# An attention kernel's last two heads: sums without transfers, tiles one at a time, output blocks behind them

## The chip, the cores and the metric

The kernel runs on one core of one Trainium2 chip. The metric is the device time of one execution in microseconds, here the median of three runs. The engines are named TensorE (PE in the profile), VectorE (DVE), ScalarE (ACT), GpSimd (POOL) and SyncE (SP, which here only issues transfers).

## What is computed

Four sequences of 2048 tokens, 512 channels, float32:

```
xn  = layernorm(x)
q   = split_heads(xn @ q_w.T + q_b, 16) / sqrt(32)     # k, v alike, not scaled
ctx = softmax(q @ k.T) @ v                             # per head, 64 heads in all
x   = x + (ctx merged) @ out_w.T + out_b + tanh(xn @ weight @ aux_weight1 @ aux_weight2 + bias)
```

## The kernel before

Two stages ahead of attention (the weights, and the projections block by block) leave q and k as a high and a low part, v, and `y` (everything of the result but the attention's share) in memory off the core. The third stage, `build_attend`, goes through 64 heads in a loop of groups of four; the last four heads (60 to 63) are written out. `more` is the number of heads that follow within the written-out part (3, 2, 1, 0 for heads 60 to 63), and 4 in the loop.

A head has 16 key tiles of 128 keys. For each tile TensorE writes four score matmuls (`scores`, L1031; a unit is one 128x512 bank) into a ring of three banks `st_bank`, ScalarE turns each into exps of `probs` (L846, in `exps`), and TensorE uses the tile (`use`, L1037: four matmuls side by side, each to 32 partitions of `pv_bank`, 8 records). For the maximum of the head after, TensorE also writes `sm_bank` (four banks, L1015), VectorE reduces it (L929), and the row of maxima is turned by TensorE (`turn_max`), negated by VectorE and sent by SyncE into the head's stack (`load_row`).

The softmax's sums: ten tiles are added by GpSimd into `pool_sum` (`add`, L781), six (`CHAINS`) by accumulating transfers into `dma_sum` (`join`, L792, issued from GpSimd's queue), then `pool_sum` is merged into `dma_sum` by one more (`merge`, L800), and TensorE sums over the partitions with a matrix of ones (`add_up`). ScalarE copies values and sums out (`copy_pv`, `copy_sums`, L853), VectorE takes reciprocals in three pieces (`recip`, L921), GpSimd scales (`scale`, L806), and SyncE stores the context (`store`, four transfers, L700). TensorE works on tiles in pairs: scores of two tiles, then the uses of the two before.

Seven of the eight `probs` buffers are reused within a head (`SLOT`); an exp that reuses one waits until the old tile is used and added. 

After the last head come 16 output blocks of 512 tokens. A block's context is loaded (L705) into the stacks of finished heads, split into `ctx_hi` (ScalarE, L864; for the first two VectorE, L970) and `ctx_lo` (VectorE, L955), multiplied by `wo_hi` and `wo_lo` in three passes (L261, 48 matmuls into four `out_banks`), `y` is added by VectorE (L963) and the result stored (L720, L717). Blocks 0 and 1 run before the last head's sums are taken from TensorE's queue, then `add_up` of head 63, then blocks 2 to 15. SyncE's queue holds head 63's store and a wait for all context stores ahead of the load of context 4. Blocks 12 to 15 are those whose sequence holds head 63.

## Time and profile before

| | |
|---|---|
| median of three runs | 4139.67 us (4138.31 to 4141.12) |
| profiled execution | 4140.99 us, span 4139.2 us |
| granted TensorE clock, mean | 0.995 |
| TensorE busy | 4072.0 us (98%) |
| VectorE busy | 3125.5 us (76%) |
| ScalarE busy | 2356.7 us (57%) |
| GpSimd busy | 3253.4 us (79%) |

The span runs from the first to the last instruction; times in the trace are counted from its start. Busy shares are means over stages with different limits. A granted clock of 1.00 is TensorE's full 2.4 GHz, half of it is the lower level of 1.2 GHz; a stretch's value is the mean over it. In a row of a timeline `xN` merges N neighbours, and a bracket gives the idle time before them and what ended it.

### The profile page before, as it was taken

The page shows a single profiled execution, that of the slowest core. Times are in us where ns is not written, and L with a number is a line of the kernel's source. Part 1 is how long each engine was busy: PE and PEld are TensorE (multiplying, and loading weights), DVE is VectorE, ACT ScalarE, POOL GpSimd, SP SyncE. Part 2 cuts the span into 40 slices and gives each one's busy share as a digit, 9 for nine tenths or more (in the row PEclk, how much of TensorE's full clock was granted, in tenths as well). Part 3 has the DMA queues.
Part 4 walks back from the last instruction along what each step waited for, and adds up shares of the span by engine and source line. Part 5 has one row for each costly group of instructions (what it writes and reads, how often), then busy time and mean ns, then how long its engine had stood idle before and what let it go on. Part 6 is the DMA issues. An engine that isn't in the chain of part 4 may idle for free.

```text
span 4139.2 us, 77715 instructions
## 1 busy us (share of the span) xinstructions
PE 4072.0 (98%) x21216; PEld 2495.7 (60%) x21216; DVE 3125.5 (76%) x5058; ACT 2356.7 (57%) x4515; POOL 3253.4 (79%) x1180
## 2 busy tenths in 40 slices
PE   8999999999999999999999999999999999999999
PEld 6888888755555555555555555555555555555467
DVE  4344334788888888888888888888888888888554
ACT  2222222266666666766666667666666766676621
POOL 1222222299999999999999999999999999999930
PEclk9999999999999999999999999999999999999999
DMA  4444445578888888888888887888888888888787
GB/s 170 158 167 162 152 147 169 161 149 175 174 178 172 174 170 175 170 173 176 176 176 172 174 170 167 175 175 175 179 169 176 172 173 172 176 176 173 156 263 262
DMA packets 246352, 722.11 MB, mean 174 GB/s; under 512 B 87392, under 2 KB 88416, under 8 KB 184544
## 3 DMA queue, kind: packets, MB, share of 16 engines
q0 software_dynamic: 55296, 402.68, 50.2%
q1 hardware_dynamic: 107648, 201.88, 14.4%
q10 hardware_dynamic: 83040, 113.01, 9.8%
q8 instruction: 185, 3.03, 0.3%
q14 instruction: 183, 1.50, 0.1%
HBM read 178.00 MB, written 136.31 MB: 76 GB/s over the span
## 4 chain that ended last, share of the span: by engine, by line
PE 46%; DMA 19%; issue 9%; POOL 3%; ACT 3%; POOLq 0%; ACTq 0%; SPq 0%; DVE 0%; DVEq 0%
PE sm_bank L1015 14%; PE pv_bank L1037 14%; PE st_bank L1031 14%; DMA dma_sum<-probs 11%; DMA dma_sum<-pool_sum 8%; ACT probs L846 3%; PE sm_bank L261 2%; POOL pool_sum L781 2%; PE sm_bank L1037 1%; PE st_bank L261 1%; POOL ctx_out L806 1%; PE sm_bank L1024 0%; POOL dma_sum L792 0%; DMA q_stack<-s_ctx 0%; ACTq L845 0%
## 5 line engine op out<-in xcount | busy, mean ns | idle before, releaser
L929 DVE TENSOR_REDUCE part_max<-sm_bank 128x1 f32<-128x512 f32 x4016 | 2442.1, 678 | 410.9 <-PE sm_bank L1015 404.1
L781 POOL TENSOR_TENSOR pool_sum<-pool_sum,probs 128x2048 f32<-128x2048 f32 x512 | 2504.8, 4892 | 16.6 <-ACT probs L846 0.7
L846 ACT ACTIVATE probs<-st_bank 128x512 f32<-128x512 f32 x3840 | 1959.8, 616 | 611.9 <-PE st_bank L1031 585.5
L1031 PE MATMUL st_bank<-q_stack,k_stack 97*128 97x512 f32 x4096 | 1649.2, 404 | 15.0 <-ACT probs L846 8.5
L1015 PE MATMUL sm_bank<-k_stack,q_stack 96*128 96x512 f32 x4016 | 1655.5, 412 | 5.3 <-issue 2.8
L1015 PEld LDWEIGHTS sm_bank<-k_stack,q_stack 96*128 96x128 f32 x4016 | 764.8, 190 | 551.9 <-DVE part_max L929 331.7
L1031 PEld LDWEIGHTS st_bank<-q_stack,k_stack 97*128 97x128 f32 x4096 | 780.5, 191 | 268.4 <-ACT probs L846 127.5
L1037 PE MATMUL pv_bank<-probs,v_pairs 128*32 128x512 f32 x7680 | 934.9, 602 | 0.0
L1037 PEld LDWEIGHTS pv_bank<-probs,v_pairs 128*32 128x32 f32 x7680 | 205.5, 110 | 455.7 <-ACT probs L846 262.8
L792 POOL DMA_DIRECT2D dma_sum<-probs x320 | 348.6, 1089 | 66.0 <-ACT probs L846 28.9
L405 POOL TENSOR_TENSOR y_out<-y_out,x_in 128x512 f32<-128x512 f32 x64 | 82.8, 1293 | 369.6 <-ACT y_out L437 365.2
L781 POOL TENSOR_TENSOR pool_sum<-probs 128x2048 f32<-128x2048 f32 x64 | 330.5, 5164 | 0.1
L921 DVE RECIPROCAL ratio<-sum_copy 128x168 f32<-128x168 f32 (+1 forms) x192 | 230.9, 1204 | 38.1 <-ACT sum_copy L853 38.1
L524 DVE SCALAR_TENSOR_TENSOR qk_lo<-proj,qk_bias,qk_hi 128x512 fp32r<-128x512 f32 x128 | 96.1, 751 | 195.0 <-ACT qk_hi L431 193.3
L431 ACT ACTIVATE qk_hi<-proj,qk_bias 128x512 fp32r<-128x512 f32 x128 | 88.1, 688 | 272.4 <-PE proj L261 272.4
L437 ACT ACTIVATE y_out<-y_out 128x512 f32<-128x512 f32 x64 | 40.5, 632 | 319.6 <-DVE y_out L513 319.6
L846 ACT ACTIVATE dma_sum<-st_bank 128x512 f32<-128x512 f32 x256 | 132.4, 603 | 132.4 <-PE st_bank L1031 132.3
L394 POOL TENSOR_TENSOR rstd<-rstd,power 128x4 f32<-128x4 f32 x15 | 15.3, 1017 | 190.5 <-DVE rstd L459 190.5
L513 DVE TENSOR_TENSOR y_out<-proj,row_bias 128x512 f32<-128x512 f32 x64 | 44.3, 692 | 121.8 <-PE proj L261 121.8
L853 ACT ACTIVATE sum_copy<-sm_bank 128x512 f32<-128x512 f32 x64 | 38.2, 597 | 168.9 <-PE sm_bank L1037 168.9
L502 DVE TENSOR_TENSOR v_out<-proj,row_bias 128x512 f32<-128x512 f32 x64 | 44.3, 692 | 104.7 <-PE proj L261 104.7
L806 POOL TENSOR_TENSOR ctx_out<-pv_copy,ratio 128x512 f32<-128x512 f32 x64 | 103.6, 1619 | 20.8 <-issue 20.8
(116 smaller groups left out, 3198.6 us busy)
## 6 DMA issues: line engine op xcount, KB each, us to landing
dma_sum<-probs POOLq DMA_DIRECT2D x320, 1024.0 KB, 8.3
dma_sum<-pool_sum POOLq DMA_DIRECT2D x64, 1024.0 KB, 10.2
q_stack<-s_q_hi ACTq DMA_DIRECT2D x122, 256.0 KB, 6.4
k_stack<-s_k_hi ACTq DMA_DIRECT2D x122, 256.0 KB, 4.4
x_in<-in_x SPq DMA_DIRECT2D x16, 1024.0 KB, 7.7
s_q_hi<-qk_hi SPq DMA_DIRECT2D x16, 1024.0 KB, 4.3
s_q_lo<-qk_lo SPq DMA_DIRECT2D x16, 1024.0 KB, 6.4
s_k_hi<-qk_hi SPq DMA_DIRECT2D x16, 1024.0 KB, 4.3
```

Source lines behind the costliest of these rows:

```text
L261: last = nc.tensor.matmul(out, a(c), b(c), start=(c == 0 and n == 0), stop=(c == CT - 1 and n == 2))
L431: nc.scalar.activation(qk_hi[:, t, g], proj[:, u % RING], ACT.Identity, bias=keep["qk_bias"][:, t, g:g + 1]).then_inc(hi_ready, 1)
L524: nc.vector.scalar_tensor_tensor(qk_lo[:, t, g], proj[:, u % RING], keep["qk_bias"][:, t, g:g + 1], qk_hi[:, t, g].bitcast(F32), ALU.add, ...
L781: nc.gpsimd.tensor_tensor(total[:], one[:], tile_at(r, kt)[:], ALU.add).then_inc(pool_added, 1)
L792: nc.gpsimd.dma_start(dma_sum[r % 2][:], tile_at(r, CHAINS[0][j])[:], accum_op=ALU.add).then_inc(joined[r % 2], DMA)
L806: nc.gpsimd.tensor_tensor(ctx_out[r % 2][:], pv_copy[r % 2][:], ratio[:], ALU.mult).then_inc(context_ready, 1)
L846: nc.scalar.activation(tile_at(r, kt)[:, q * BLK:(q + 1) * BLK], st_bank[:, st_place(kt * QB + q)], ACT.Exp, scale=SCALE).then_inc(probs_r ...
L921: nc.vector.reciprocal(ratio[:, columns], sum_copy[r % 2][:, columns]).then_inc(recip_ready, 1)
L929: nc.vector.tensor_reduce(part_max[:, k:k + 1], sm_bank[:, sm_place(k)], AX.X, ALU.max).then_inc(max_scores_read, 1)
L1015: nc.tensor.matmul(sm_bank[:, sm_place(k)], q_st[r][0:ROWS, q * P:(q + 1) * P], k_st[r][0:ROWS, b * BLK:(b + 1) * BLK], start=True, stop=T ...
L1031: nc.tensor.matmul(st_bank[:, st_place(u)], k_st[r][0:ROWS + 1, kt * P:(kt + 1) * P], q_st[r][0:ROWS + 1, q * BLK:(q + 1) * BLK], start=Tr ...
L1037: last = nc.tensor.matmul(bank[q * DH:(q + 1) * DH, :], left, right[:, q * BLK:(q + 1) * BLK], start=start, stop=stop)
```

## The change

The last two heads and the start of the output stage are rewritten; heads 0 to 61 keep their order except for the points named.

- **TensorE.** From tile 12 of head 62 on (`end_of_heads`, 20 steps) it takes tiles one at a time: four scores, then the use of the tile two before. The scores go round five banks (`end_ring`: three of `st_bank`, two of `sm_bank` whose maxima are over). The row of maxima for head 63 is turned at the first step.
- **Sums of head 62**: joins as before, but no merge; `add_up_both` spreads `dma_sum` and `pool_sum` by two series of matmuls.
- **Sums of head 63**: no transfers. TensorE sums seven tiles (`PE_TILES`) with ones right behind their use into the bank of the maxima (`last_sum`); GpSimd adds the other nine (`add_last`, eight adds), and `add_up_last` adds that before block 3. GpSimd's scale of head 62 stands before its fifth add.
- **Output.** The first matmul group of block 0 stands before the uses of tiles 14 and 15; blocks 0 to 3 are written out, 4 to 13 are a loop, 14 and 15 written out. Output banks, result buffers and the buffers of `y` are others.
- **SyncE.** `wo_hi` and `wo_lo` are loaded behind head 60's store instead of head 61's. Contexts 0 to 3 and `y` 0 and 1 are loaded before head 62's store. Head 63's store stands behind block 3; the wait for all context stores behind block 9, before context 12 is loaded.
- **VectorE.** Head 61's reciprocals follow the last maxima; the first two contexts are split before head 62's reciprocals; head 63's stand around results 3.

The diff, cut to its core (moved or renamed lines that the prediction doesn't speak of are left out):

```diff
--- before.py
+++ after.py
@@ -51,7 +51,17 @@
...
-RESULT_TILES = [9, 11]
...
+LAST = ALL_HEADS - 1
+END_TILE = 12
+PE_TILES = [0, 1, 2, 5, 8, 10, 13]
+LAST_POOL = [kt for kt in range(KT) if kt not in PE_TILES]
+LAST_ADDS = len(LAST_POOL) - 1
+LAST_SCALE = 4
+RESULT_TILES = [8, 10]
+EARLY_BLOCKS = 4
+LAST_CONTEXT = (BATCH - 1) * TB
...
+def in_end(h, kt):
+
+    return isinstance(h, int) and (h == LAST or (h == LAST - 1 and kt >= END_TILE))
+
+
+def end_unit(h, u):
+
+    return (h - LAST + 1) * UNITS + u - END_TILE * QB
...
-        y_in = [tiled(pool_sum[0]), tiled(q_st[3]).bitcast(F32)]
+        y_in = [tiled(pool_sum[0]), tiled(dma_sum[0])]
...
-        out_banks = [sm_bank[:, b] for b in range(SM_BANKS) if b != sm_place("sum")] + [st_bank[:, 0]]
+        last_sum = sm_bank[:, sm_place("max")]
+        out_banks = [sum_bank] + [sm_bank[:, b] for b in range(SM_BANKS) if b not in (sm_place("sum"), sm_place("max"))]
+        out_banks += [st_bank[:, 0]]
+        end_free = [max(k for k in range(UNITS) if sm_place(k) == b) for b in range(SM_BANKS)]
+        end_ring = [st_place(END_TILE * QB + i) for i in range(ST_BANKS)]
+        end_ring += [ST_BANKS + b for b in range(SM_BANKS) if b not in (sm_place("sum"), sm_place("max"))]
...
+        def score_bank(h, u):
+
+            if not in_end(h, u // QB):
+                return st_bank[:, st_place(u)]
+            place = end_ring[end_unit(h, u) % len(end_ring)]
+            return st_bank[:, place] if place < ST_BANKS else sm_bank[:, place - ST_BANKS]
...
-            def body(h, r, more, following):
-                if more == 0:
-                    for n in range(2):
-                        sp.wait_ge(lo_ready, n + 1)
-                        load_context(n + 2, n)
-                    sp.wait_ge(tile_used, PRIME + h * KT + KT)
-                    load_y(1, 1)
-                    store_result(0, 0)
-                    load_y(2, 0)
-                    store_result(1, 1)
-                    load_y(3, 1)
-                if more >= 2:
-                    load_row(following + 1, (r + 2) % GROUP)
-                if more == 1:
-                    sp.wait_ge(sums_ready, PRIME + h + 1)
-                    load_y(0, 0)
-                store(h, r)
-                if more == 2:
-                    sp.wait_ge(first["v_stored"], V_STORED)
-                    sp.wait_ge(first["y_stored"], Y_STORED)
-                    sp.dma_start(wo_hi[:].bitcast(F32), dram["wo_hi"].rearrange("(r p) c -> p r c", p=P)).then_inc(w_loaded, DMA)
-                    sp.dma_start(wo_lo[:].bitcast(F32), dram["wo_lo"].rearrange("(r p) c -> p r c", p=P)).then_inc(w_loaded, DMA)
-                    for n in range(2):
-                        load_context(n, n)
-
-            heads(sp, body)
-            for s in context_stored:
-                sp.wait_ge(s, PRIME + CTX_DMAS * DMA * ALL_HEADS // 2)
-
...
-            block_pairs(sp, output)
+            def body(h, r, more, following):
+                if more >= 2:
+                    load_row(following + 1, (r + 2) % GROUP)
+                if more == 1:
+                    sp.wait_ge(sums_ready, PRIME + h)
+                    for n in range(2):
+                        load_context(n, n)
+                    for n in range(2):
+                        sp.wait_ge(lo_ready, n + 1)
+                        load_context(n + 2, n)
+                    sp.wait_ge(sums_ready, PRIME + h + 1)
+                    for n in range(2):
+                        load_y(n, n)
+                if more >= 1:
+                    store(h, r)
+                if more == 3:
+                    sp.wait_ge(first["v_stored"], V_STORED)
+                    sp.wait_ge(first["y_stored"], Y_STORED)
+                    sp.dma_start(wo_hi[:].bitcast(F32), dram["wo_hi"].rearrange("(r p) c -> p r c", p=P)).then_inc(w_loaded, DMA)
+                    sp.dma_start(wo_lo[:].bitcast(F32), dram["wo_lo"].rearrange("(r p) c -> p r c", p=P)).then_inc(w_loaded, DMA)
+
+            heads(sp, body)
+            for n in range(2):
+                store_result(n, n)
+                load_y(n + 2, n)
+            for n in range(2, EARLY_BLOCKS):
+                output(n, n % 2, True)
+            store(LAST, LAST % GROUP)
+            block_pairs(sp, output, EARLY_BLOCKS, LAST_CONTEXT - 2)
+            for s in context_stored:
+                sp.wait_ge(s, PRIME + CTX_DMAS * DMA * ALL_HEADS // 2)
+            block_pairs(sp, output, LAST_CONTEXT - 2, BLOCKS - 2)
...
+            def add_last(i):
+
+                total, kt = pool_sum[LAST % 2], LAST_POOL[i + 1]
+                if i == 0:
+                    pool.wait_ge(sums_ready, PRIME + LAST - 1)
+                pool.wait_ge(probs_ready, PRIME + LAST * UNITS + QB * (kt + 1))
+                one = tile_at(LAST, LAST_POOL[0]) if i == 0 else total
+                if i:
+                    pool.wait_ge(pool_added, PRIME + LAST * POOL_ADDS + i)
+                nc.gpsimd.tensor_tensor(total[:], one[:], tile_at(LAST, kt)[:], ALU.add).then_inc(pool_added, 1)
...
+                if more >= 2:
+                    for i in range(POOL_ADDS):
+                        if i == SCALE_ADD:
+                            scale(h, r)
                         sum_up(following, (r + 1) % GROUP, i)
-                    if i == MERGE_AFTER:
-                        merge(h, r)
+                        if i == MERGE_AFTER:
+                            merge(h, r)
+                elif more == 1:
+                    for i in range(LAST_ADDS):
+                        if i == LAST_SCALE:
+                            scale(h, r)
+                        add_last(i)
+                else:
+                    scale(h, r)
...
-                        if old in POOL_TILES:
+                        if not back and isinstance(h, int) and h == LAST:
+                            if old in LAST_POOL:
+                                act.wait_ge(pool_added, PRIME + h * POOL_ADDS + max(1, LAST_POOL.index(old)))
+                        elif old in POOL_TILES:
                             act.wait_ge(pool_added, PRIME + h * POOL_ADDS - back * POOL_ADDS + adds_after(old))
...
+                bank = last_sum if isinstance(h, int) and h == LAST else sum_bank
+                copy_bank(h, r, bank, sum_copy, sums_ready, PRIME + h + 1, sums_copied)
...
+                    high(3, 1)
...
             heads(act, body)
-            high(3, 1)
-            block_pairs(act, lambda n, par, ahead: high(n + 2, par) if ahead else None)
+            for n in range(4, EARLY_BLOCKS + 2):
+                high(n, n % 2)
+            block_pairs(act, lambda n, par, ahead: high(n + 2, par), EARLY_BLOCKS, BLOCKS - 2)
...
-                if more == 0:
+                if more >= 3:
+                    rest(following + 1, sums_of=(h, r))
+                    begin(following + 2, sums_of=(h, r))
+                elif more == 2:
+                    rest(following + 1, last=True)
+                    negate(following + 1)
+                    for piece in range(len(RECIPS)):
+                        recip(h, r, piece)
+                elif more == 1:
                     for n in range(2):
                         high(n, n)
                         low(n, n)
-                    dve.wait_ge(tile_used, PRIME + h * KT + KT)
-                    dve.wait_ge(pool_added, PRIME + h * POOL_ADDS + adds_after(RESULT_TILES[1]))
-                    results(0, 0)
-                    low(2, 0)
-                    results(1, 1)
                     for piece in range(len(RECIPS)):
                         recip(h, r, piece)
-                else:
-                    rest(following + 1, units=more >= 2, sums_of=(h, r))
-                    begin(following + 2, units=more >= 3, new=more >= 2, sums_of=(h, r))

             heads(dve, body)
+            for n in range(EARLY_BLOCKS):
+                if n:
+                    low(n + 1, (n + 1) % 2)
+                if n == EARLY_BLOCKS - 1:
+                    recip(LAST, LAST % GROUP, 0)
+                results(n, n % 2)
+            recip(LAST, LAST % GROUP, 1)
+            recip(LAST, LAST % GROUP, 2)
...
+                if not in_end(h, kt):
+                    pe.wait_ge(probs_ready, PRIME + h * UNITS + st_units_before(u))
+                else:
+                    unit = end_unit(h, u)
+                    if unit >= len(end_ring):
+                        pe.wait_ge(probs_ready, PRIME + h * UNITS + u - len(end_ring) + 1)
+                    elif unit < ST_BANKS:
+                        pe.wait_ge(probs_ready, PRIME + h * UNITS + st_units_before(u))
+                    else:
+                        pe.wait_ge(max_scores_read, PRIME + LAST * UNITS + end_free[end_ring[unit] - ST_BANKS] + 1)
+                nc.tensor.matmul(score_bank(h, u), k_st[r][0:ROWS + 1, kt * P:(kt + 1) * P],
...
+                last = spread(pv_bank, v_sb[r // 2][:, kt, (r % 2) * DH:(r % 2 + 1) * DH], tile, kt == 0, kt == KT - 1)
+                if isinstance(h, int) and h == LAST and kt in PE_TILES:
+                    if kt == PE_TILES[0]:
+                        pe.wait_ge(max_row_ready, ALL_HEADS)
+                    last = spread(last_sum, ones[:], tile, kt == PE_TILES[0], False)
+                last.then_inc(tile_used, 1)
...
+            def add_up_both(h, r):
+
+                pe.wait_ge(joined[r % 2], landed(h, len(CHAINS[0]) - 1))
+                spread(sum_bank, ones[:], dma_sum[r % 2], True, False)
+                pe.wait_ge(pool_added, PRIME + h * POOL_ADDS + POOL_ADDS)
+                spread(sum_bank, ones[:], pool_sum[r % 2], False, True).then_inc(sums_ready, 1)
+
+            def add_up_last():
+
+                pe.wait_ge(pool_added, PRIME + LAST * POOL_ADDS + LAST_ADDS)
+                spread(last_sum, ones[:], pool_sum[LAST % 2], False, True).then_inc(sums_ready, 1)
...
+            def end_of_heads():
+
+                tiles = [(LAST - 1, kt) for kt in range(KT)] + [(LAST, kt) for kt in range(KT)]
+                for i in range(END_TILE, len(tiles)):
+                    h, kt = tiles[i]
+                    for q in range(QB):
+                        scores(h, h % GROUP, kt, q)
+                    before, used = tiles[i - 2]
+                    use(before, before % GROUP, used)
+                    if i == END_TILE:
+                        turn_max(LAST, False)
+                    if h == LAST and kt == CUT - 1:
+                        add_up_both(LAST - 1, (LAST - 1) % GROUP)
...
+                if more == 0:
+                    return
                 r1 = (r + 1) % GROUP
-                for p in range(CUT // 2, KT // 2):
+                for p in range(CUT // 2, (KT if more >= 2 else END_TILE) // 2):
...
+                if more == 1:
+                    end_of_heads()
...
             pe.wait_ge(consts_ready, 1)
             heads(pe, body, extra=1)
             pe.wait_ge(w_loaded, 2 * DMA)
-            pe.wait_ge(max_row_ready, ALL_HEADS)
-            output(0, 0, True)
-            output(1, 1, True)
-            add_up(ALL_HEADS - 1, (ALL_HEADS - 1) % GROUP, 0)
-            block_pairs(pe, output)
+            pe.wait_ge(sums_copied, PRIME + LAST)
+            pe.wait_ge(lo_ready, 1)
+            output_part(0, 0, 0)
+            use(LAST, LAST % GROUP, KT - 2)
+            use(LAST, LAST % GROUP, KT - 1)
+            for j in range(1, JT):
+                output_part(0, 0, j)
+            for n in range(1, EARLY_BLOCKS):
+                if n == EARLY_BLOCKS - 1:
+                    add_up_last()
+                output(n, n % 2, True)
+            block_pairs(pe, output, EARLY_BLOCKS, BLOCKS - 2)
+            last_blocks(output)
```

## Rows read from the trace of the kernel before

**Rows 1.** Windows; busy us (and count) per engine, granted clock, DMA share, GB/s
```profile
3600.00:3647.60 47.60, 47.49 (x264) 26.56 (x263) 41.80 (x69) 33.23 (x66) 46.93 (x16) 1.00 0.89 183
3882.65:3949.07 66.42, 62.47 (x269) 20.35 (x265) 20.99 (x11) 41.48 (x82) 61.76 (x20) 0.87 0.84 204
...
3979.60:3993.00 13.40, 13.40 (x49) 10.88 (x50) 9.14 (x10) 1.91 (x1) 3.14 (x1) 0.81 0.79 274
4004.70:4135.60 130.90, 130.85 (x576) 108.13 (x576) 57.44 (x61) 21.09 (x11) 0.00 (x0) 1.00 0.81 276
```
**Rows 2.** Timeline of TensorE, last two heads: start us, us, line, operation, tiles
```profile
3882.65 0.98 PE L1031 MATMUL st_bank<-q_stack,k_stack 97*128 97x512 f32 x3
3883.92 2.46 PE L1031 MATMUL st_bank<-q_stack,k_stack 97*128 97x512 f32 x5 [0.29 <-ACT probs L846]
...
3888.16 0.28 PE L1024 MATMUL sm_bank<-ident,row_max 128*16 128x128 f32 x1
...
3936.72 3.53 PE L1037 MATMUL pv_bank<-probs,v_pairs 128*32 128x512 f32 x16
```
**Rows 3.** Timeline of ScalarE, one pair of tiles
```profile
3883.27 4.03 ACT L846 ACTIVATE probs<-st_bank 128x512 f32<-128x512 f32 x8 [1.64 <-PE st_bank L1031]
```
**Rows 4.** Chain of work that ended last: start us, us, what
```profile
3858.25 7.92 DMA dma_sum<-probs
...
3906.21 11.16 DMA dma_sum<-probs
...
3993.11 6.59 DMA q_stack<-s_ctx
...
4135.60 0.69 DVE probs L963
```
**Rows 5.** Timeline of TensorE at full clock, steady heads
```profile
3832.55 1.93 PE L1037 MATMUL pv_bank<-probs,v_pairs 128*32 128x512 f32 x16
3834.41 0.50 PE L1015 MATMUL sm_bank<-k_stack,q_stack 96*128 96x512 f32 x1
3834.75 0.40 PE L1031 MATMUL st_bank<-q_stack,k_stack 97*128 97x512 f32 x1
...
3838.34 1.92 PE L1037 MATMUL pv_bank<-probs,v_pairs 128*32 128x512 f32 x16
...
3875.49 1.04 PE L1037 MATMUL sm_bank<-dma_sum,ones 128*32 128x512 f32 x8
```
**Rows 6.** Timeline of GpSimd, from head 61's sums on
```profile
3863.40 1.48 POOL L800 DMA_DIRECT2D dma_sum<-pool_sum  x1
...
3901.73 4.78 POOL L781 TENSOR_TENSOR pool_sum<-pool_sum,probs 128x2048 f32<-128x2048 f32 x1
...
3943.17 11.50 POOL L781 TENSOR_TENSOR pool_sum<-pool_sum,probs 128x2048 f32<-128x2048 f32 x2
...
3984.77 3.14 POOL L806 TENSOR_TENSOR ctx_out<-pv_copy,ratio 128x512 f32<-128x512 f32 x1 [20.75 <-issue]
```
**Rows 7.** Window of 5 us in head 62's first half
```profile
3860.00:3865.00 5.00, 4.85 (x28) 2.33 (x27) 3.64 (x7) 2.90 (x7) 5.00 (x3) 1.00 1.04 210
```
**Rows 8.** Timeline of TensorE's weight loads: the wait of head 62's sums
```profile
3925.39 0.15 PEld L1037 LDWEIGHTS sm_bank<-dma_sum,ones 128*32 128x32 f32 x4 [0.97 <-DMA dma_sum<-pool_sum]
```
**Rows 9.** Timeline of SyncE's DMA queue: when transfers were issued
```profile
3902.05 4.27 SPq L700 DMA_DIRECT2D s_ctx<-ctx_out  x4
...
3907.43 0.52 SPq L705 DMA_DIRECT2D q_stack<-s_ctx  x1
```
**Rows 10.** Timeline of VectorE, first context blocks
```profile
3934.38 3.80 DVE L970 CAST q_stack<-q_stack 128x2048 fp32r<-128x2048 f32 x1 [2.98 <-DMA q_stack<-s_ctx]
3938.21 6.51 DVE L955 TENSOR_TENSOR k_stack<-q_stack 128x2048 fp32r<-128x2048 f32 x1
...
3981.26 3.37 DVE L921 RECIPROCAL ratio<-sum_copy 128x168 f32<-128x168 f32 x3
3984.54 2.23 DVE L955 TENSOR_TENSOR k_stack<-k_stack,q_stack 128x2048 fp32r<-128x2048 f32 x1
```

More of the change, by code:

```diff
@@ L939, in begin, with rest @@
                     maxima(s, k, units, sums_of)
-            def rest(s, units=True, sums_of=None):
+            def rest(s, units=True, sums_of=None, last=False):
                 for k in range(BEGIN, UNITS):
-                    maxima(s, k, units, sums_of)
+                    maxima(s, k, units, None if last else sums_of)
                 if units:
@@ L993, in output @@
                 results(n, par)
-            block_pairs(dve, output)
+            block_pairs(dve, output, EARLY_BLOCKS, BLOCKS - 2)
+            last_blocks(output)
         @block.tensor
@@ L1064, in both_scores @@
                     s, ahead, k0 = following + 1, 2, PER_TILE * (kt - KT + AHEAD)
-                if k0 == TURN_UNIT and more >= 1:
-                    turn_max(following, more >= 2)
+                if k0 == TURN_UNIT and more >= 2:
+                    turn_max(following)
                 for q in range(QB):
```

33 lines of the change are left out of this document (13 added, 20 removed).

## The prediction

> **What bounds the kernel now.** I read the windows by stage first, then TensorE's timeline, then the chain that ended last. The windows [rows 1] show three kinds of stretch. In a steady head TensorE is busy 47.49 of 47.60 us at granted clock 1.00, and GpSimd 46.93: the two are level. From 3882.65 to 3949.07, which the change rewrites, the granted clock is 0.87. From 4004.70 to 4135.60 twelve output blocks follow each other with no gap, 130.9 / 12 = 10.9 us each. Block 2, at 3979.60, takes 13.4 us at clock 0.81.
>
> What sets 3882.65 to 3949.07 is seen in TensorE's timeline [rows 2]. The maxima matmuls are over there. Two tiles of scores are written as three matmuls, then five at 0.49 us each, every one behind an exp that frees one of three banks; then both tiles are used. A pair lasts 3888.16 - 3882.65 = 5.51 us. ScalarE has eight exps in 4.03 us and then sits idle 1.5 to 1.6 us [rows 3], since the whole burst of uses stands ahead of the next score. Neither engine is full: each waits for the other in turn.
>
> The chain [rows 4] runs through GpSimd and the accumulating transfers into `dma_sum`, then through the store and reload of context, and from 4004.7 through TensorE alone. TensorE's work ends at 4135.60; VectorE's last add and the last store bring the span to 4139.2. Between blocks 1 and 2 TensorE is idle: blocks 0 and 1 end at 3949.07 + 2 x 10.9 = 3970.9 and block 2 starts at 3979.6 [rows 1], with one spread of sums between.
>
> **The scores and uses.** I lay the new TensorE order out from 3882.65, where the old and the new code part. It has 20 tile steps (tiles 12 to 15 of head 62, 16 of head 63): four scores, then the use of the tile two back. Prices come from full clock [rows 5]. Sixteen score matmuls and both changes of kind take 3838.34 - 3834.41 = 3.93 us; a change costs 3834.75 - 3834.41 = 0.34 us, so the others are (3.93 - 0.68) / 14 = 0.23 us. Four scores with both changes are 0.34 + 0.34 + 2 x 0.23 = 1.14 us. Two uses are 3834.41 - 3832.55 = 1.86 us, one 0.93. A step is 2.05 us (I drop the last hundredths). ScalarE needs half of 4.03, 2.0 us, so TensorE just sets the pace. Do five banks suffice? A score must wait for the exp five units back; an exp starts 0.62 us after its score [rows 2, 3], and the eight in 4.03 us are seven distances of 0.49 and one duration of 0.60. The loop of five units costs 1.25 us against 2.5 us of exps: they suffice. Twenty steps: 41.0 us.
>
> Head 63's sums for seven tiles become TensorE spreads of the same form as a use. A spread of sums took 1.04 us, the part that the next matmul does not overlap 0.97 [rows 5]: 7 x 0.97 = 6.8 us. Head 62's sums are two spreads, not one (`pool_sum` is no longer merged): 1.9 us. The use of head 63's tile 0, in the seventh step, waits for ScalarE's copy of head 62's values, which follows the exps of tile 1. TensorE comes to it at 3882.65 + 6 x 2.05 + 1.14 = 3896.1. The exps begin 0.62 us after the sixth step, at 3893.5, and end 2.1 us later, the copy half a microsecond behind: 3896.1 to 3896.2. I take 0.1 us. The last two uses are 1.9 us, the last sums' spread 1.0 us.
>
> **What must be ready in time.** GpSimd's adds of head 62 end at 3906.5 [rows 6]. Then come eight adds of head 63 at 4.78 us and one scale. Exps of tiles 10, 14 and 15 reuse slots that adds 1, 2 and 3 free, at about 3911, 3916 and 3921; by the steps they are due at 3919, 3929 and 3931. Head 63's tile 7 needs the last add of head 62, 3906.5, due at 3909. So no step waits. The scale of head 62 waits for its reciprocals, which VectorE makes behind four passes over the first context blocks (below), to about 3938; a scale and four adds later it is 3959, or 3964 at the 3.14 and 5.75 us that they took beside VectorE [rows 6]. TensorE wants the sum before block 3, at about 3969 (3934 and three blocks, and what follows). Hidden, with 5 to 10 us to spare; if that cover is gone, each microsecond counts in full.
>
> **The loads of `wo`.** SyncE issues them one head earlier, behind head 60's store. Head 61's is issued at 3902.05 + 4.27 = 3906.3 [rows 9], so head 60's ends one head of 47.6 us earlier, at 3858.7. There head 62's first join and head 61's merge are in flight and the transfer engines are saturated, share 1.04 [rows 7]. Uncontended that join took 7.92 us; with 4 MB of loads beside it a join took 11.16 [rows 4]. The merge was issued at 3863.40 [rows 6]; with the same 4 MB beside it head 62's merge, issued one add after 3906.5 and so at 3911.3, held TensorE until 3925.39 [rows 8], 14 us. Now 2 MB: head 61's merge would land between 3863.4 + 7.9 = 3871.3 and 3863.4 + 14 = 3877.4, while TensorE wants it at 3875.49. The cost is 0 to 1.9 us; I take 1.0. GpSimd loses 2 to 4 us to late joins, which the slack above mostly covers.
>
> **Contexts and `y`.** The loads of context 0 and 1 still follow head 61's store, so are issued at about 3907 as before [rows 9], but nothing large is in front of them: before, context 0 landed only when VectorE began at 3934.38 [rows 10], 27 us. Alone a load took 6.59 us [rows 4]. I expect 3914 to 3917. VectorE then splits it: 3.80 + 6.51 us while GpSimd adds, but 2.23 us for the same subtraction with GpSimd idle [rows 10]. The first block is ready at 3927, the second at 3934; TensorE wants them at 3934 and 3947. `y` is issued behind the second and lands around 3943, an estimate from that 6.59 us with two loads ahead, before block 1 needs block 0's banks.
>
> **The output stage.** Sixteen blocks of 10.9 us, 174.1 us at the finer value of 10.88 between equal matmuls. Against it stands the store of the last context. Its reciprocals follow results 3, so with block 4 starting at B they end at B + 3.1 (two of the three pieces of 3.37 us [rows 10] behind 0.7 us); the scale takes at most 3.14 us [rows 6]; four stores take 4.27 us to issue [rows 9]; only then is context 6 loaded. From such a load to the block that uses it were 4004.70 - 3993.11 = 11.6 us [rows 1, 4]. Block 6 can start at B + 22.1 at the latest and is due at B + 21.8. With a quicker scale there is nothing, with a load of 7.92 us as the join's instead of 6.59 it is 1.6 us. I take nothing, nearest to the first. The wait for all stores stands before context 12 is loaded, some 60 us later: free.
>
> **The sum.** 41.0 + 6.8 + 1.9 + 0.1 + 1.9 + 1.0 + 174.1 + 1.0 = 227.8 us after 3882.65: TensorE ends at 4110.45 in place of 4135.60, 25.15 us less, with the same tail. The profiled execution took 4140.99 us for a span of 4139.2, 1.3 us above the median of 4139.67; the difference is taken off the median: 4114.5 us.
>
> **The rivals.**
> - *The sum holds*, 4114.5 us: chance 0.61. Its own range is 4111 to 4119: without contention 4113.5, at ScalarE's 2.0 us a step 4112.5, the other way 0.9 for the `wo` loads and 1.6 for context 6, 4117.0; a microsecond or two more on both sides for the transitions.
> - *The granted clock falls in the tile-by-tile stretch too.* In [rows 1] the clock was 0.87 over 66 us in which TensorE was busy 94%, and a pair's uses took 3.53 us at the lower level (1.2 GHz) against 1.9 at 2.4 GHz [rows 2]. For it: the engine still changes kind each step and meets ScalarE closely. Against: the short waits of 0.29 us after three scores, present in every pair before the fall, are gone, and a steady head with the same kinds of matmul and no such waits holds 1.00. At 0.87 the 52.7 us of work before block 0 and for the last sums take 60.6: 4122.4 us, chance 0.17. The Trainium skill's page "TensorE: Matmul & The Clock Gate", section "A second HAM failure mode: psum-queue depth-cycling", says that micro-idles between groups of matmuls that cycle through PSUM banks make the clock swing; the rows of the pairs agree, and by that rule a five-bank ring that waits often would keep this cost.
> - *GpSimd or a transfer is late.* Joins with loads beside them, a slow context 0, or reciprocals behind VectorE's contended passes. If context 0 takes 27 us again it is split at 3934.4 + 3.8 + 2.2 = 3940.4 at the earliest, and block 0 starts 6.5 us late: 4121 us, chance 0.13. For it: the chain already runs through joins. Against: the merges and five joins of head 63 are gone from the queue. The Trainium skill's "GPSIMD Engine Reference", section "Specifications", says that GpSimd shares its SBUF interfaces with VectorE instructions that have two SBUF inputs; 6.51 against 2.23 us agrees, and by that rule the adds are slowed as well.
> - *Slower than before:* the clock stays at its lower level through the whole stretch. Uses then cost 1.77 us instead of 0.93, and the 52.7 us become about 98, so 4159 us. It decides from 25 / 0.85 = 29 us of full-clock work spent at that level. The old stretch had a quarter of its time there. Chance 0.03; 0.06 is left for a gain of the sum that other waits mostly take back, half of it within 0.2%.
>
> **The range.** 4109 to 4128 holds the first three cases and their bounds. Within 0.2% is 4131.4 to 4148.0, about what a measurement can tell from no change. Faster: 0.61 + 0.17 + 0.13 + 0.02 = 0.93; same 0.04, slower 0.03.
>
> **What would show it.** Right: clock 1.00 and TensorE over 97% busy between the first tile step and block 0; steps of 2.05 us, 3.0 with sums; block 0 starting near 3934; no idle time before block 2 or 4; a wait of about 1 us at head 61's sums. Wrong: exps that wait for `pool_sum` or for joins in head 63; TensorE waiting before the spread of the last sums or before block 6; a granted clock under 1.00 in the tile steps.

## The result and the profile after

| | kernel before | changed kernel |
|---|---|---|
| median (4 runs of each) | 4140.4 us (4138.31 to 4143.34) | 4116.7 us (4113.47 to 4121.45) |
| profiled execution, span | 4140.99, 4139.2 us | 4121.45, 4119.6 us |
| first tile step to block 0's first matmul | 66.42 us [rows 1] | 50.33 us |
| from there to the end of the span | 190.1 us (4139.2 - 3949.07) | 180.9 us |

The ratio is 0.9943, 95% interval 0.9926 to 0.996: 23.7 us less, where 25.15 were forecast, and a median of 4116.7 us for the forecast's 4114.5. The profiled execution is the slowest of its four. Its first tile step comes at 3888.41, 5.8 us later than in the profile of before; from that step to the end it needs 231.2 us against 256.55, 25.35 less. The sum is judged on that stretch; the time ahead of it is taken up at the end.

The windows of the changed kernel, which answer to [rows 1] (same columns):
```profile
3888.41:3938.74 50.33, 50.33 (x318) 19.03 (x314) 23.47 (x9) 42.15 (x82) 45.35 (x12) 1.00 0.50 126
3938.74:4116.40 177.66, 177.64 (x792) 144.46 (x792) 80.22 (x83) 27.92 (x16) 24.72 (x6) 1.00 0.79 267
```
Sixteen blocks, the last two uses and the last sums' spread follow the steps with 0.02 us of idle time, all at clock 1.00: the gap before block 2, block 2's 13.4 us and the 0.87 of [rows 1] are gone. TensorE's timeline, which answers to [rows 2, 5]; a matmul's end overlaps the next start, so steps are read from starts:
```profile
3891.70 1.06 PE L1117 MATMUL pv_bank<-probs,v_pairs 128*32 128x512 f32 x8
3892.70 0.73 PE L1111 MATMUL sm_bank<-q_stack,k_stack 97*128 97x512 f32 x2
3893.26 0.62 PE L1111 MATMUL st_bank<-q_stack,k_stack 97*128 97x512 f32 x2
3893.81 1.07 PE L1117 MATMUL pv_bank<-probs,v_pairs 128*32 128x512 f32 x8
3894.81 0.50 PE L1111 MATMUL st_bank<-q_stack,k_stack 97*128 97x512 f32 x1
...
3929.57 1.07 PE L1117 MATMUL pv_bank<-probs,v_pairs 128*32 128x512 f32 x8
3930.45 1.04 PE L1117 MATMUL sm_bank<-probs,ones 128*32 128x512 f32 x8
3931.42 0.74 PE L1111 MATMUL sm_bank<-q_stack,k_stack 97*128 97x512 f32 x2
...
3973.65 1.06 PE L1117 MATMUL sm_bank<-pool_sum,ones 128*32 128x512 f32 x8
```
A step is 3893.81 - 3891.70 = 2.11 us (2.12 over several), a use alone 3892.70 - 3891.70 = 1.00. With sums behind it a use takes 0.88 and the sums 0.97, so a spread adds 0.86. No row has a bracket: the last sums' spread did not wait. GpSimd and VectorE say why, against [rows 6, 10]:
```profile
3917.75 16.73 POOL L855 TENSOR_TENSOR pool_sum<-pool_sum,probs 128x2048 f32<-128x2048 f32 x3
3941.30 1.28 POOL L844 TENSOR_TENSOR ctx_out<-pv_copy,ratio 128x512 f32<-128x512 f32 x1 [6.83 <-issue]
3942.54 20.73 POOL L855 TENSOR_TENSOR pool_sum<-pool_sum,probs 128x2048 f32<-128x2048 f32 x4
```
```profile
3918.76 4.67 DVE L1032 CAST q_stack<-q_stack 128x2048 fp32r<-128x2048 f32 x1 [24.33 <-DMA q_stack<-s_ctx]
3923.46 6.57 DVE L1017 TENSOR_TENSOR k_stack<-q_stack 128x2048 fp32r<-128x2048 f32 x1
3929.95 5.61 DVE L1032 CAST q_stack<-k_stack 128x2048 fp32r<-128x2048 f32 x1
3935.59 2.29 DVE L1017 TENSOR_TENSOR k_stack<-k_stack,q_stack 128x2048 fp32r<-128x2048 f32 x1
3937.80 3.37 DVE L983 RECIPROCAL ratio<-sum_copy 128x168 f32<-128x168 f32 x3
```
Context 0 is there at 3918.76. GpSimd's three adds beside VectorE's passes take 5.6 us each (16.73 / 3), then GpSimd waits 6.83 us for the reciprocals; its last four adds, during which VectorE is busy less than half of the time, take 5.2 each. GpSimd ends at 3963.27 and the sum is wanted at 3973.65. SyncE's queue, which answers to [rows 9]:
```profile
3908.57 4.18 SPq L735 DMA_DIRECT2D s_ctx<-ctx_out  x4
3912.79 0.97 SPq L740 DMA_DIRECT2D q_stack<-s_ctx  x1
...
3992.12 1.74 SPq L735 DMA_DIRECT2D s_ctx<-ctx_out  x4
3994.43 0.43 SPq L740 DMA_DIRECT2D q_stack<-s_ctx  x1
```
Context 0 needs 3918.76 - 3912.79 = 6.0 us from issue, where 27 us passed before. The four stores of head 63 take 1.74 us to issue, not 4.27.

### The profile page after: what moved, and what is told of

The parts are those of the page before. It is cut to its first block, busy times and chain, and to the rows that moved or that the text cites. A ratio compares the mean times of both kernels' runs of the same rounds, so it can differ in the third digit from the quotient of the medians.

```text
span 4119.6 us, 77775 instructions
## 1 busy us (share of the span) xinstructions
PE 4060.4 (99%) x21280; PEld 2484.5 (60%) x21280; DVE 3122.5 (76%) x5058; ACT 2357.2 (57%) x4515; POOL 3243.9 (79%) x1172
## 4 chain that ended last, share of the span: by engine, by line
PE 46%; DMA 19%; issue 10%; ACT 3%; POOL 2%; POOLq 0%; ACTq 0%; DVE 0%; DVEq 0%
PE sm_bank L1086 13%; PE pv_bank L1117 13%; PE st_bank L1111 13%; DMA dma_sum<-pool_sum 10%; DMA dma_sum<-probs 9%; PE sm_bank L281 3%; ACT probs L905 3%; PE sm_bank L1117 2%; PE st_bank L281 1%; POOL pool_sum L819 1%; POOL ctx_out L844 1%; POOL dma_sum L830 0%; PE sm_bank L1095 0%; PE sm_bank L1111 0%; ACTq L904 0%
## 5 line engine op out<-in xcount | busy, mean ns | idle before, releaser
L819 POOL TENSOR_TENSOR pool_sum<-pool_sum,probs 128x2048 f32<-128x2048 f32 x504 | 2462.7, 4886 | 17.6 <-ACT probs L905 2.2
L1111 PE MATMUL st_bank<-q_stack,k_stack 97*128 97x512 f32 x4064 | 1628.9, 402 | 11.7 <-ACT probs L905 5.4
L1111 PEld LDWEIGHTS st_bank<-q_stack,k_stack 97*128 97x128 f32 x4064 | 772.2, 190 | 251.3 <-ACT probs L905 114.2
L844 POOL TENSOR_TENSOR ctx_out<-pv_copy,ratio 128x512 f32<-128x512 f32 x64 | 102.0, 1594 | 32.5 <-issue 32.5
```

What stands on the lines that cost most here:

```text
L819: nc.gpsimd.tensor_tensor(total[:], one[:], tile_at(r, kt)[:], ALU.add).then_inc(pool_added, 1)
L844: nc.gpsimd.tensor_tensor(ctx_out[r % 2][:], pv_copy[r % 2][:], ratio[:], ALU.mult).then_inc(context_ready, 1)
L1111: nc.tensor.matmul(score_bank(h, u), k_st[r][0:ROWS + 1, kt * P:(kt + 1) * P], q_st[r][0:ROWS + 1, q * BLK:(q + 1) * BLK], start=True, sto ...
```

## The experiments

"Stretch" is first tile step to block 0's first matmul, "rest" from there to the end of the span. A ratio is to the kernel before on the same chip. Stretch, rest and clock are read from one profiled execution of each kernel. The edits are shown against the changed kernel, cut to the lines that matter.

**The changed kernel again** (c1), no edit.

> The changed kernel once more, for a tighter ratio and to see what its first profile can't tell: that execution was the slowest of four, and one head ahead of all changed code had a 4.1 us wait on ScalarE. If that wait is chance, this profile has none before head 61, and the span is 4 to 6 us shorter (4113 to 4116). If the new code brings it, it stands at the same head again. From the first score of tile 12 of head 62 to block 0: 50.3 us as before, plus or minus 0.5.

Measured: median 4118.98 us of six (4109.94 to 4123.74), ratio 0.9941 (0.9925 to 0.9957); stretch 50.22, rest 181.0, clock 1.00. In the three profiles of this kernel (the changed kernel's, c1 and f2 below) the stretch is 50.21 to 50.33 us and the rest 180.9 to 181.0, while the spans are 4115.6 to 4120.4: what differs between these executions lies ahead of the stretch. The wait of ScalarE that the expectation asks about is there again, at the same head (the last section).

**Three banks** (c2): the steps stay, the ring shrinks.
```diff
-        end_ring += [ST_BANKS + b for b in range(SM_BANKS) if b not in (sm_place("sum"), sm_place("max"))]
```


> Tile by tile, but the scores go round three banks as before the change. If the ring's length sets the pace: the fourth score waits for the first exp, so a step is 1.27 to that score, 0.31 and 0.93, 2.51 us in place of 2.12; 20 steps are 8 us longer, about 58 us to block 0. If ScalarE or TensorE sets the pace whatever the banks: no more than 1 us longer. If short waits of this kind bring the granted clock down: 58 us and 5 to 8 more, clock 0.87 to 0.90 in the stretch.

**Pairs, five banks** (c3): the order of before, the rest of the change as it is.
```diff
-                for i in range(END_TILE, len(tiles)):
-                    h, kt = tiles[i]
-                    for q in range(QB):
-                        scores(h, h % GROUP, kt, q)
-                    before, used = tiles[i - 2]
-                    use(before, before % GROUP, used)
+                for i in range(END_TILE, len(tiles), 2):
+                    for h, kt in tiles[i:i + 2]:
+                        for q in range(QB):
+                            scores(h, h % GROUP, kt, q)
+                    for before, used in tiles[i - 2:i]:
+                        use(before, before % GROUP, used)
```


> Five banks, but tiles in pairs: eight scores, then two uses. If the banks do it: the eighth score waits for the third exp, 2.25 us after the first; with 0.31 and 1.86 a pair is 4.42 to 4.5 us in place of 4.24, so 2 to 3 us more over ten pairs, about 53 us to block 0. If the order tile by tile does it, a pair costs 5.5 us as before the change: 13 us more. Clock 1.00 by the first.

**Pairs, three banks** (c4): both edits.

> Pairs and three banks, that is the scores and uses as before the change, with all the rest of the change (sums, output blocks, transfers) kept. A pair is 5.5 us in place of 4.24: 12.7 us more, 63 us to block 0, and with the clock falling as it did before 4 to 8 us more. The rest of the gain, about 25 less 13 to 20 us, must then stay: 5 to 12 us faster than the kernel before. If instead the order of scores is worth little, it stays within 3 us of the changed kernel.

| | median us | ratio (95%) | stretch | rest | clock in the stretch |
|---|---|---|---|---|---|
| c1 tiles, 5 banks | 4118.98 | 0.9941 (0.9925 to 0.9957) | 50.22 | 181.0 | 1.00 |
| c2 tiles, 3 banks | 4131.25 | 0.9969 (0.9958 to 0.998) | 61.43 | 181.0 | 1.00 |
| c3 pairs, 5 banks | 4123.97 | 0.9954 (0.9939 to 0.9969) | 52.93 | 181.0 | 1.00 |
| c4 pairs, 3 banks | 4134.56 | 0.9984 (0.9972 to 0.9995) | 62.73 | 180.95 | 1.00 |

The stretch as a window in c2, c3 and c4, one block each, and TensorE's timeline in c2:
```profile
3888.41:3949.84 61.43, 55.53 (x317) 18.93 (x313) 22.53 (x11) 42.29 (x82) 57.68 (x16) 1.00 0.56 159
```
```profile
3884.16:3937.09 52.93, 52.93 (x317) 20.72 (x314) 23.04 (x10) 41.34 (x82) 46.88 (x13) 1.00 0.50 126
```
```profile
3886.82:3949.55 62.73, 59.81 (x318) 20.69 (x314) 26.67 (x11) 41.24 (x82) 54.17 (x15) 1.00 0.56 157
```
```profile
3893.79 0.97 PE L1110 MATMUL st_bank<-q_stack,k_stack 97*128 97x512 f32 x3
3895.05 0.50 PE L1110 MATMUL st_bank<-q_stack,k_stack 97*128 97x512 f32 x1 [0.30 <-ACT probs L904]
3895.49 1.06 PE L1116 MATMUL pv_bank<-probs,v_pairs 128*32 128x512 f32 x8
3896.49 0.96 PE L1110 MATMUL st_bank<-q_stack,k_stack 97*128 97x512 f32 x3
```
The banks carry it: with pairs, two more are worth 62.73 - 52.93 = 9.8 us, with tiles 61.43 - 50.22 = 11.2. Tile order is worth 1.3 us with three banks and 2.7 with five. The medians differ from c1's by 12.3 us (c2), 5.0 (c3) and 15.6 (c4); the intervals of the ratios are 9 to 13 us wide, so they bear the order out, but not the single microseconds, which rest on one profile each. c3 shows no idle time, 52.93 of 52.93 us busy. Rows of TensorE's uses and of its weight loads (PEld) show where a pair loses time all the same:
```profile
3891.38 1.92 PE L1117 MATMUL pv_bank<-probs,v_pairs 128*32 128x512 f32 x16
...
3895.83 1.93 PE L1117 MATMUL pv_bank<-probs,v_pairs 128*32 128x512 f32 x16
```
```profile
3894.42 0.19 PEld L1111 LDWEIGHTS st_bank<-q_stack,k_stack 97*128 97x128 f32 x1 [0.19 <-ACT dma_sum L905]
3894.91 0.19 PEld L1111 LDWEIGHTS st_bank<-q_stack,k_stack 97*128 97x128 f32 x1 [0.30 <-ACT dma_sum L905]
3895.39 0.19 PEld L1111 LDWEIGHTS sm_bank<-q_stack,k_stack 97*128 97x128 f32 x1 [0.30 <-ACT dma_sum L905]
```
The weight loads of the sixth, seventh and eighth score of a pair start 0.48 to 0.49 us apart, which is the pace of the exps, where scores that don't wait start 0.23 apart; idle time of 0.19 to 0.30 us stands before each and ends with an exp. A pair takes 3895.83 - 3891.38 = 4.45 us where two steps take 4.24. In c2 a step is 3896.49 - 3893.79 = 2.70 us, more than the 2.51 that was expected, and its stretch 61.43 us for 58: each fourth score waits 0.30 us for an exp, and starts 1.26 us after the first where 0.34 + 2 x 0.23 = 0.80 would do. The other part of the miss was not taken apart. c4 against the kernel before is what the rest of the change gives (sums, output order, transfers, and the clock that came with them), and it is read with the next two runs.

**The kernel before again, and pairs without TensorE's sums** (d1, no edit, and d2; one execution each, as are d3 and d4 below). d2 is c4 without the seven spreads of head 63, so its sums for head 63 lack these seven tiles.
```diff
-                    last = spread(last_sum, ones[:], tile, kt == PE_TILES[0], False)
```


> The kernel before once more, for its profile: where its granted clock falls. If the fall belongs to what TensorE does there, the clock is again 0.80 to 0.90 between the first pair without maxima and block 0 (66.4 us in the first profile), and block 2 follows at about 0.8. If it was chance, the clock is 1.00 there and the stretch 60 to 62 us.

> Pairs and three banks once more, and TensorE's seven spreads of head 63's sums are left out (its softmax sums then hold GpSimd's nine tiles alone; part of the computation is missing). The run with the spreads held clock 1.00 at the same short waits. If the spreads kept it up, by filling the stretch, the clock now falls some 20 us into the stretch as in the kernel before, to 0.85 to 0.93 over it, and the stretch is 58 to 62 us in place of 62.7 - 6.8 = 55.9. If the accumulating transfers or their waits brought it down before, the clock stays at 1.00 and the stretch is 55.9 us.

Measured: d1 4138.81 us (another execution of the kernel before, timed beside d1 to d4, took 4144.79), stretch 64.05; d2 4126.53 us, stretch 63.31, rest 181.0. Windows of d1, then windows and one pair's uses of d2:
```profile
3880.82:3900.00 19.18, 18.04 (x83) 6.56 (x79) 2.96 (x5) 14.66 (x30) 18.89 (x6) 1.00 0.55 111
3900.00:3910.00 10.00, 9.23 (x35) 2.99 (x38) 0.00 (x0) 6.06 (x12) 10.00 (x6) 0.71 0.79 158
```
```profile
3880.40:3900.00 19.60, 18.45 (x84) 6.74 (x80) 3.56 (x4) 15.10 (x31) 19.31 (x7) 1.00 0.50 102
3900.00:3943.71 43.71, 41.92 (x178) 13.06 (x178) 23.18 (x7) 26.21 (x53) 35.35 (x9) 0.84 0.57 181
```
```profile
3925.91 3.36 PE L1116 MATMUL pv_bank<-probs,v_pairs 128*32 128x512 f32 x16
```
Both hold 1.00 up to 3900 and fall behind it. d2 has no joins for head 63, so joins are not needed for a fall. Against c4 it has 7 x 0.86 = 6.0 us less to do and takes 0.6 us more: the work that was taken out came back as clock, 0.89 for 1.00, with uses of 3.36 us.

Do the seven spreads keep the clock up, then? Shorter windows of the kernel before and of d2, and the first spread in c4's timeline, say only in part:
```profile
3902.00:3904.00 2.00, 2.00 (x10) 0.63 (x14) 0.00 (x0) 1.77 (x4) 2.00 (x2) 0.69 1.07 217
```
```profile
3904.00:3906.00 2.00, 2.00 (x5) 0.74 (x4) 0.00 (x0) 2.00 (x6) 2.00 (x2) 0.94 0.91 206
3906.00:3908.00 2.00, 2.00 (x13) 0.46 (x16) 0.00 (x0) 1.03 (x3) 2.00 (x1) 0.50 0.52 128
```
```profile
3907.82 1.04 PE L1116 MATMUL sm_bank<-dma_sum,ones 128*32 128x512 f32 x8
```
A mean of 0.94 or 0.69 between the levels 1.00 and 0.50 puts the fall at 3905.8 in d2 and at 3902.8 in the kernel before. So in d2 the clock falls 25.4 us after the first tile step, where c4 already has spreads behind it (the first 3907.82 - 3886.82 = 21.0 us after the step). In the kernel before and in d1 it falls after 19.9 to 20.1 us, and neither c4 nor d2 falls there, with the same order of scores and uses, the same short waits, and no spread of head 63 yet. So the spreads may account for d2 against c4, but not for the first fall of the kernel before; what spared c4 and d2 that one is open, and the joins and the other transfers that they lack remain a rival. With one profile of each of c4 and d2, chance in when the clock falls is not ruled out either, and c4's ten executions have mean granted clocks from 0.995 to 0.999, of which the profiled one is among the highest: the others may have lost clock here or elsewhere.

**The last sums before block 1** (d4): is GpSimd's cover real, and what does it cost if it is gone?
```diff
-                if n == EARLY_BLOCKS - 1:
+                if n == 1:
```


> GpSimd's part of head 63's sums is asked for before block 1, not before block 3, that is 21.8 us earlier. In the changed kernel's profile GpSimd ended 24.5 us after block 0's start and was asked after 35.0 us. If TensorE's queue order is the cover, it now waits 24.5 - 13.2 = 11.3 us before block 1, the granted clock falls for the start of block 1 (2 to 3 us more, as at block 2 of the kernel before), and the span grows by 11 to 14 us. If GpSimd speeds up without VectorE beside it, 8 to 11 us.

Measured: 4131.32 us, stretch 50.23, rest 195.7 instead of 180.95, so +14.75. TensorE's timeline, and a window right behind it:
```profile
3959.61 1.93 PE L1117 MATMUL sm_bank<-pool_sum,ones 128*32 128x512 f32 x8 [12.53 <-POOL pool_sum L855]
```
```profile
3960.00:3975.00 15.00, 15.00 (x62) 11.09 (x55) 2.77 (x4) 0.24 (x1) 0.00 (x0) 0.86 0.01 1
```
The wait is 12.5 us, and 2.2 us more come from TensorE's clock after it: 0.86 for 15 us, 15.00 x 0.14 = 2.1. Here the wait cost more than its own time. The expectation had 11.3 us of waiting and 11 to 14 in all.

**The output weights later** (d3; g2 is the same kernel, timed over six executions).
```diff
-                if more == 3:
+                if more == 2:
                     sp.wait_ge(first["v_stored"], V_STORED)
```


> The two loads of wo behind head 61's store, as before the change, ahead of contexts 0 and 1. With 4 MB on SyncE's queue but no joins of head 63 beside them, context 0 should land 12 to 16 us after its issue, near 3928 by this kernel's clock of 3913 for the issue, in place of 6; split by 3938 to 3940, so TensorE waits 0 to 3 us before block 0. If the move was needed, it is as before, 27 us and a wait of 6 us or more with block 0 at the lower clock. At head 61's sums nothing changes (the change's loads cost nothing there), GpSimd's wait of 1.5 us before head 62's second join goes.

**A lighter end** (f1; f2 is the changed kernel beside it). TensorE sums five tiles, GpSimd adds the other eleven in ten adds; head 62's reciprocals stand between the two splits, and `y` 0 and 1 are loaded before context 3. g1 is f1 with the weights later.
```diff
-PE_TILES = [0, 1, 2, 5, 8, 10, 13]
+PE_TILES = [1, 2, 5, 8, 10]
-LAST_POOL = [kt for kt in range(KT) if kt not in PE_TILES]
+LAST_POOL = [3, 4, 6, 7, 9, 11, 12, 13, 14, 15, 0]
...
-                    for n in range(2):
-                        high(n, n)
-                        low(n, n)
+                    high(0, 0)
+                    low(0, 0)
                     for piece in range(len(RECIPS)):
                         recip(h, r, piece)
+                    high(1, 1)
+                    low(1, 1)
```


> Two more tiles of head 63 (13 and 0) are added by GpSimd instead of TensorE; head 62's reciprocals come before the second context is split, so that GpSimd does not wait for them (6.8 us in the changed kernel's profile), and y 0 and 1 are loaded before context 3. TensorE loses two spreads of 0.86 to 0.97 us and nothing waits: block 0 starts 48.4 to 48.6 us after the first tile step in place of 50.3, GpSimd ends about 28 us after block 0's start, asked at 35. Median 1 to 2 us under the changed kernel of this call, within what its measurement can tell. If GpSimd is late instead, TensorE waits before the spread of the last sums; if y is late, before block 1.

> The changed kernel beside it on the same chip: 0.993 to 0.995 of the kernel before; block 0 starts 50.2 to 50.4 us after the first tile step, and the last 231.2 us of the span from there are the same within 0.5.

> The lighter end of f1 (five tile steps by TensorE, ten adds by GpSimd) with the output weights loaded behind head 61's joins instead of ahead of them. Theory: the two savings add. From head 60's last copy of its sums to the first tile step 30.5 us as in d3 (36.0 in f1, 31.6 in the changed kernel beside it), no wait of head 61's sums spread for its merge; stretch from the first tile step to block 0 48.5 us, from block 0 to the end 181.0; GpSimd's last add ends 31 to 34 us after block 0 starts and is asked for after 35. Time about 3.7 us under the changed kernel, ratio to the kernel before 0.992 to 0.9935. Rival: the 4 MB that now lie ahead of head 61's context in the queue make the context land late, so that the split, the reciprocals and GpSimd's scale start later; GpSimd then ends past 35 us after block 0 and the last sums' spread waits 1 to 4 us, and the time is no better than f1's (ratio 0.9938 or more).

> The changed kernel with the output weights loaded behind head 61's joins, timed beside g1. Theory: the stretch and all behind it as in the changed kernel (50.2 and 180.9 us), from head 60's last copy to the first tile step 30.5 us instead of a mean near 32, so the time is 1 to 2 us under the changed kernel: ratio to the kernel before 0.9935 to 0.994, and g1 1.7 us under it. Rival: what the weights cost ahead of head 61 comes back as a wait at block 0 or block 1 for the late context, and the time is the changed kernel's, ratio 0.9945.

| | median us (runs) | ratio (95%) | stretch | rest | head 61's first part |
|---|---|---|---|---|---|
| d3 weights later | 4115.95 (1) | one execution | 50.21 | 180.9 | 30.56 |
| f1 lighter end | 4118.87 (6) | 0.9938 (0.9925 to 0.995) | 48.47 | 181.0 | 36.02 |
| f2 changed kernel | 4122.46 (6) | 0.995 (0.9936 to 0.9964) | 50.21 | 180.94 | 31.56 |
| g1 both | 4112.75 (5) | 0.992 (0.9901 to 0.9938) | 48.48 | 183.6 | 30.50 |
| g2 weights later | 4114.87 (6) | 0.9926 (0.9907 to 0.9945) | 50.25 | 181.0 | 30.53 |

The last column is from ScalarE's copy of head 60's values to the first tile step, where head 61's sums are spread: 30.50 us before (3882.65 - 3852.15). TensorE's timeline and a window of f1, then TensorE's timeline of g2:
```profile
3879.75 1.39 PE L1119 MATMUL sm_bank<-dma_sum,ones 128*32 128x512 f32 x8 [2.60 <-DMA dma_sum<-pool_sum]
```
```profile
3882.00:3889.63 7.63, 7.63 (x32) 4.50 (x30) 5.59 (x9) 4.67 (x8) 6.35 (x3) 0.66 0.51 105
```
```profile
3881.21 1.04 PE L1117 MATMUL sm_bank<-dma_sum,ones 128*32 128x512 f32 x8
```
With the weights' 2 MB ahead, head 61's merge is late in f1 and TensorE waits 2.60 us, after which the clock falls to 0.66. With them behind head 61's store, as in before, neither is there: before, d1, d3, g1 and g2 have 30.50 to 30.56 us. In g2 and d3 nothing came back at block 0: in d3 context 0 landed 3917.53 - 3906.99 = 10.5 us after its issue with the weights in front of it, against 6.0 without them and 27 before, and its expectation of 0 to 3 us of waiting was not met. So the move of the weights, which the prediction took to be needed for context 0, cost about 2 us and bought nothing that these profiles show. f1 itself is 3.6 us under f2 by the medians, with overlapping intervals; its stretch is 1.7 us shorter, as expected.

g1 met its rival halfway. TensorE's timeline, a window right behind the wait, and GpSimd's timeline:
```profile
3970.18 1.06 PE L1119 MATMUL sm_bank<-pool_sum,ones 128*32 128x512 f32 x8 [2.54 <-POOL pool_sum L856]
```
```profile
3970.18:3982.00 11.82, 11.82 (x56) 9.08 (x56) 5.24 (x5) 2.40 (x2) 0.00 (x0) 1.00 0.71 239
```
```profile
3933.97 2.08 POOL L845 TENSOR_TENSOR ctx_out<-pv_copy,ratio 128x512 f32<-128x512 f32 x1 [5.57 <-issue]
3936.01 27.55 POOL L856 TENSOR_TENSOR pool_sum<-pool_sum,probs 128x2048 f32<-128x2048 f32 x5
3963.71 6.41 POOL L856 TENSOR_TENSOR pool_sum<-pool_sum,dma_sum 128x2048 f32<-128x2048 f32 x1
```
GpSimd ends at 3970.12, 37.55 us after block 0, and is asked for after 35. This wait of 2.54 us cost its own time alone (rest 183.6 us for 181.0): the clock behind it is 1.00. From the first tile step g1 needs 232.1 us and g2 231.2, so in the profiles the lighter end gives nothing once the weights are moved. The medians are 2.1 us apart the other way, with overlapping intervals. Which of the two is faster stays open. That both are under the changed kernel is likely, from head 61's first part, 30.5 us where the changed kernel's place of the weights has 32.5 on average. The ratios point the same way but don't show it: both intervals overlap f2's, and f2 was timed on another chip.

## Why the prediction was right

Each step against its measurement in the changed kernel's profile; the terms add to 226.8 us without the weights' 1.0, and TensorE needed 228.0 (3888.41 to 4116.40).

- **Steps:** 20 x 2.12 = 42.4 for 41.0. The mis-sized part is the use. With scores on both sides it costs 0.99, not half of a pair's 1.86: a use that is followed by its own kind takes 0.87 to 0.88, and only the one before a score takes 0.99, which the halving hid.
- **Sums of seven tiles:** 7 x 0.86 = 6.0 for 6.8, and head 62's two spreads 1.7 for 1.9: right behind a use the same 0.11 us is not paid. These errors, 1.4 us too little and 1.0 too much, nearly cancel, which is luck.
- **The copy's wait:** none for 0.1. Last two uses 1.85 for 1.9, last sums' spread 1.0 for 1.0.
- **Blocks:** 10.88 us each from block 4 on as forecast. What is left of the difference, under 1 us, lies in block 0, whose matmuls are parted by two uses, and in the last matmul's own end.
- **Five banks suffice:** right, four scores take 3893.81 - 3892.70 = 1.11 us for the 1.14 priced, so none waited for a bank; c2 and c4 show what three cost.
- **Clock:** 1.00 in the stretch of all 11 profiles that have TensorE's sums. The rival that it falls did not come. Of the two reasons given, "the short waits are gone" was not needed: c2 and c4 keep waits of 0.30 us in every step or pair and hold 1.00 too. What does hold the clock up is not settled (d2 above), so the forecast of 1.00 came true without its reason being shown. The Trainium skill's page "TensorE: Matmul & The Clock Gate", section "A second HAM failure mode: psum-queue depth-cycling", would have the clock swing there; d2 and the kernel before agree with it, c2 and c4 do not.
- **GpSimd:** it ended 74.9 us after the first tile step (forecast 76.4 to 81.4) and was asked for after 85.2 (86.4). d4 shows that the cover was real and that without it the 12.5 us count in full, and 2.2 us of clock on top.
- **Context 0 and `y`:** context 0 landed 30.4 us after the first tile step (forecast 31.4 to 34.4), `y` 57.5 (60.4). The rival of a late transfer did not come.
- **Context 6:** its split ends at 4003.87 and block 6 starts at 4007.59, 3.7 us of slack where the bounds gave -0.3: the four stores took 1.74 us to issue, not 4.27.
- **The weights:** the mis-sized term. Nine profiles with the new place have 30.53 to 36.02 us for head 61's first part, a mean of 32.5, so 2.0 us for the 1.0 taken and 5.5 for the 1.9 set as the bound. The bound counted a late merge; the clock that falls after the wait was left out. The changed kernel's own profile has 30.53 us, no cost at all, so the term can't be read from it alone.

So without the weights 25.35 us are measured for the forecast's 26.15 (1.2 more work, a tail 0.4 shorter); the weights take 2.0 for 1.0, which leaves 23.35 beside the medians' 23.7.

Where the 25.35 us come from, by the profile of c4: 12.5 from banks and order, of which the banks are 9.8; 12.85 from the rest. By the medians the rest is less: c4 is 8.7 us under the kernel before, with an interval of 2 to 12, and the weights' 2.0 are in it, so the profile's 12.85 - 2.0 = 10.85 lies near its upper end. In c4 that rest is 9.1 us behind block 0 (190.1 - 181.0: no reload behind a store, no slow block 2) and 3.7 us ahead of it, although eight spreads, 6.9 us, came in there (the last two uses, 1.9 us, went behind block 0's start). The prediction had the total, but its pairs lost their time to waits alone; here a part of it was clock, 0.87 to 0.92 in the stretch of before and 1.00 in c4's profile.

## What to carry to other kernels

A ring of banks that is too short makes two engines take turns; count the loop of bank, exp and score, not each engine's load, and find the free banks first, the order of work second. Where an engine's clock sags beside idle gaps, taking work away can gain nothing (c4 and d2, one profile each: 6.0 us less work, 0.6 us more time). A wait of TensorE is to be priced with a range that holds the slow stretch that may follow it: 12.5 us cost 14.75 (d4) and 2.6 us cost 5.5 (f1), but another of 2.54 us cost 2.6 (g1).

## What the runs showed of the hardware beside that

Where the loop over groups of heads ends and the written-out head 60 begins, ScalarE stops for 2.0 to 4.6 us in every one of the 14 profiles, before and changed, with nothing in the profile to release it. The place is the same: in all of them the exp behind the wait starts 3.26 to 3.28 us plus the wait after ScalarE's copy of head 59's values. ScalarE's timelines of the kernel before and of the changed one, and then two windows of the changed one:
```profile
3808.90 5.70 ACT L846 ACTIVATE probs<-st_bank 128x512 f32<-128x512 f32 x11 [3.50 <-issue]
```
```profile
3812.03 3.54 ACT L905 ACTIVATE probs<-st_bank 128x512 f32<-128x512 f32 x7 [4.10 <-issue]
```
```profile
3804.66:3815.00 10.34, 8.49 (x42) 4.97 (x43) 7.11 (x12) 6.12 (x13) 10.34 (x6) 0.99 0.79 166
3815.00:3830.00 15.00, 15.00 (x67) 7.89 (x67) 10.00 (x17) 8.80 (x18) 14.86 (x6) 0.78 0.99 202
```
TensorE's score after it waited 0 to 2.4 us (1.26 in before's profile, 1.85 in this one), and here the clock then fell to 0.78 for 15 us. Head 60 took 53.2 us in this profile, 50.0 before and 48.45 in d1: that is most of why the changed kernel's first tile step comes 5.8 us late in it, and it can be a part of the spread of 7 to 18 us between executions of one kernel. What ScalarE waits for was not tried.
